# Moving the division by the softmax sum from the attention stage into the loads of the output projection

## The reference

```python
h = _layernorm(x, axis=-1) * (1 + ca) + sa
...
scores = jnp.einsum('bhqd,bhkd->bhqk', q, k) / jnp.sqrt(jnp.float32(D))
scores = jnp.where(causal[None, None], scores, jnp.finfo(x.dtype).min)
attn = jax.nn.softmax(scores, axis=-1)
out = jnp.einsum('bhqk,bhkd->bhqd', attn, v)
out = out.transpose(0, 2, 1, 3).reshape(b, s, H * D)
return out @ Wo
...
x = x + ga * attention(h)
```

## Time and profile before

| | us |
|---|---|
| executions of the kernel before | 2085.73, 2091.81, 2093.32 (median 2091.81) |
| the profiled execution | 2089.15 |
| its span, first to last instruction | 2087.3 |
| mean granted TensorE clock, share of full speed | 0.947 |
| TensorE matmuls busy in the span | 1812.4 (87%) |
| VectorE, ScalarE, GpSimd busy | 1277.5, 1149.3, 953.9 |
| attention lasts, in the span | about 109 to 1425 |
| output projection | about 1425 to 1679 |
| feed-forward | 1679 to the end |

### The profile page before, as it was taken

One profiled execution on the slowest core, in us unless ns is written; L12 is line 12 of the kernel. 1 busy time (PEld: TensorE's weight loads), 2 busy tenths in 40 slices (PEclk: granted clock), 3 DMA queues, 4 the chain that ended last, 5 costly groups with the idle time before them and its releaser, 6 DMA issues. The chain is left out here.

```text
span 2087.3 us, 32037 instructions
## 1 busy us (share of the span) xinstructions
PE 1812.4 (87%) x9585; PEld 1503.0 (72%) x9585; DVE 1277.5 (61%) x2079; ACT 1149.3 (55%) x2307; POOL 953.9 (46%) x773
## 2 busy tenths in 40 slices
PE   8489989979989989989988998984888869999997
PEld 7377778767768777777777886873766647777776
DVE  6367768768767767767777876783222246454543
ACT  4267767767757767767776776783222234233221
POOL 0236556556556556655655665662000014444443
PEclk8799999999999999999999999997999979999999
DMA  6134334243244334333433433435444310101000
GB/s 239 29 89 117 79 102 120 79 113 102 78 111 107 82 95 108 102 90 100 119 89 99 115 81 94 111 88 171 148 149 146 121 56 1 46 1 46 1 26 21
DMA packets 174968, 191.48 MB, mean 92 GB/s; under 512 B 31408, under 2 KB 117688, under 8 KB 174784
## 3 DMA queue, kind: packets, MB, share of 16 engines
q1 hardware_dynamic: 162496, 170.36, 29.2%
q10 hardware_dynamic: 12288, 18.88, 3.1%
HBM read 86.12 MB, written 31.74 MB: 56 GB/s over the span
## 5 line engine op out<-in xcount | busy, mean ns | idle before, releaser
L816 DVE TENSOR_TENSOR p_lo<-ps_b,p_hi 128x512 fp32r<-128x512 f32 x576 | 394.5, 686 | 190.2 <-ACT p_hi L746 186.7
L746 ACT CAST p_hi<-ps_b 128x512 fp32r<-128x512 f32 x576 | 337.4, 588 | 232.1 <-PE ps_b L702 227.0
L759 ACT ACTIVATE p<-ps_b,negm 128x640 f32<-128x640 f32 (+7 forms) x512 | 381.6, 749 | 123.5 <-DVE negm L824 119.2
L824 DVE TENSOR_REDUCE negm<-ps_b 128x1 f32<-128x640 f32 (+7 forms) x512 | 377.4, 747 | 116.4 <-PE ps_b L694 112.5
L702 PE MATMUL ps_b<-ident,p 128*128 128x128 f32 x2304 | 360.5, 280 | 19.4 <-issue 11.0
L692 PE MATMUL ps_b<-k_hh,q_hl 128*128 128x512 f32 (+3 forms) x768 | 273.0, 355 | 82.4 <-DMA q_hl<-rot_x 53.5
L714 PE MATMUL ps_b<-p_hi,v_hl 128*128 128x512 f32 x576 | 280.7, 487 | 14.8 <-ACT o_sb L752 14.2
L702 PEld LDWEIGHTS ps_b<-ident,p 128*128 128x128 f32 x2304 | 255.9, 143 | 51.2 <-issue 16.8
L693 PE MATMUL ps_b<-k_l,q_hl 128*128 128x512 f32 (+3 forms) x768 | 262.5, 354 | 0.0
L898 POOL TENSOR_TENSOR o_sb<-o_sb,rd_all 64x512 f32<-64x512 f32 x128 | 164.2, 1282 | 177.4 <-DMA rd_all<-reciprocals 175.3
L692 PEld LDWEIGHTS ps_b<-k_hh,q_hl 128*128 128x128 f32 x768 | 149.4, 194 | 128.1 <-issue 57.4
(11 more groups left out here) (139 smaller groups left out, 3311.9 us busy)
## 6 DMA issues: line engine op xcount, KB each, us to landing
rot_x<-rot_s SPq DMA_DIRECT2D x320, 64.0 KB, 2.0
q_hl<-rot_s SPq DMA_DIRECT2D x128, 128.0 KB, 2.4
q_hl<-rot_x SPq DMA_DIRECT2D x128, 128.0 KB, 2.4
rd_all<-reciprocals SPq DMA_DIRECT2D x128, 128.0 KB, 3.0
o_low<-o_sb SPq DMA_DIRECT2D x128, 128.0 KB, 2.2
attention_out<-o_sb SPq DMA_DIRECT2D x128, 128.0 KB, 2.5
o_raw<-attention_out SPq DMA_DIRECT2D x32, 512.0 KB, 6.3
wf<-in_L_ffn_w_gate_up ACTq DMA_DIRECT2D x32, 256.0 KB, 3.1
```

The costliest lines, as they stand in the source:

```text
L746: act.copy(p_hi[:, T % P_RING, :], ps[:, T_BANK + T % 2, :]).then_inc(phi_ready, 1)
L759: act.activation(p_32[:, parity, h, column * P:column * P + nk], s, ACT.Exp, bias=negm[:, k:k + 1], scale=1.0, accum_out=den[:, parity, k: ...
L816: dve.tensor_tensor(p_lo[:, T % P_RING, :], ps[:, T_BANK + T % 2, :], p_hi[:, T % P_RING, :].bitcast(F32), ALU.subtract).then_inc(plo_read ...
L824: dve.tensor_reduce(negm[:, k:k + 1], s, AX.X, ALU.max, negate=True).then_inc(max_ready, 1)
```

## The change

In attention GpSimd's multiply, `rd_all` and `spread_den` are gone; the store follows the add and stands one step earlier. The reciprocals of all heads and queries are kept in DRAM, at a place of their own for each. In the projection each piece gets a second ring buffer `o_by`, filled by two DMAs that read the reciprocals of two heads' rows into 64 partitions each; GpSimd multiplies `o_raw` by `o_by` in place, and ScalarE's cast waits for that instead of for the load.

```diff
@@ attention
-        rd_all = sb("rd_all", [D, 512], F32)
...
-        pairs_out = Events(rd_out, [64] * PAIRS, None)
+        pairs_out = [Events(s, [64] * (PAIRS // 2), None) for s in rd_out]
...
+            rden_g = rden_dram.rearrange("(g h) (u i q) -> g u i h q", u=B, g=KVH, q=P)
...
-                blocks_s.await_(sp, g, n)
+                blocks_a.await_(sp, g, n)
...
             def save_den(g, n):
+                big = BIG[n % 4]
                 pairs_flip.await_(sp, g, n)
                 for b in range(P // DEN_COLS):
-                    rows = slice(DEN_COLS * b, DEN_COLS * b + DEN_COLS)
-                    sp.dma_start(rden_dram[n % 2, :, rows], rd_turned[rows.start:rows.start + len(ROWS), n % 2, :]).then_inc(rd_out, 16)
-
-            def spread_den(g, n):
-                if n % 2 == 0:
-                    pairs_out.await_(sp, g, n // 2)
-                row = rden_dram[n // 2 % 2, GQ * (n % 2):GQ * (n % 2) + GQ, :].rearrange("(o h) q -> o (h q)", o=1)
-                sp.dma_start(rd_all[:], row.broadcast_to([D, GQ * P])).then_inc(rd_in[n % 2], 16)
+                    cols = slice(DEN_COLS * b, DEN_COLS * b + DEN_COLS)
+                    to = rden_g[bass.ds(g, 1), n // 4, 7 - big:big + 1:2 * big - 7, :, cols]
+                    sp.dma_start(to.rearrange("g i h q -> (g i) h q"),
+                                 rd_turned[cols.start:cols.start + len(ROWS), n % 2, :]).then_inc(rd_out[n % 2], 16)
...
-                for g, n in body.blocks(T, LAG + 5):
+                for g, n in body.blocks(T, LAG + 4):
                     store(g, n)
                 for g, n in body.pairs(T, 2):
                     save_den(g, n)
-                for g, n in body.pairs(T, 6):
-                    spread_den(g, 2 * n)
-                for g, n in body.blocks(T, LAG + 5):
-                    if n % 2 == 0:
-                        spread_den(g, n + 1)
...
-                               accum_out=den[:, parity, k:k + 1]).then_inc(p_ready, 1)
+                               accum_out=den[:, parity, (k + GQ) % 8:(k + GQ) % 8 + 1]).then_inc(p_ready, 1)
...
-                    pairs_out.await_(dve, g, n - 2)
+                    pairs_out[n % 2].await_(dve, g, n // 2 - 1)
...
-                for g, n in body.blocks(T, LAG + 4):
-                    blocks_a.await_(pool, g, n)
-                    blocks_rd[n % 2].await_(pool, g, n // 2)
-                    pool.tensor_tensor(o_sb[0:D, n % 2, :], o_sb[0:D, n % 2, :], rd_all[:], ALU.mult).then_inc(o_scaled, 1)
@@ project_outputs
+        o_by = sb("o_by", [P, O_RING, PIECE, HALF], F32)
...
+            by_n = rden_dram.rearrange("(k o) (n i t) -> n i o k t", n=NCH, i=2, o=2)
...
                 sp.dma_start(o_raw[:, s % O_RING], ot_n[bass.ds(n, 1), :, i, k].rearrange("n p k t -> (n p) k t")).then_inc(o_in[s % O_RING], 16)
+                for o in range(2):
+                    src = by_n[bass.ds(n, 1), i, o, k].broadcast_to([D, PIECE, HALF])
+                    sp.dma_start(o_by[D * o:D * o + D, s % O_RING], src).then_inc(by_in[s % O_RING], 16)
...
-                    act.wait_ge(o_in[s % O_RING], n * (16 * NPC // O_RING) + 16 * (s // O_RING + 1))
+                    act.wait_ge(o_divided, n * NPC + (s + 1))
...
+            def body(n, first):
+                for s in range(NPC):
+                    slot, turn = s % O_RING, s // O_RING + 1
+                    pool.wait_ge(o_in[slot], n * (16 * NPC // O_RING) + 16 * turn)
+                    pool.wait_ge(by_in[slot], n * (32 * NPC // O_RING) + 32 * turn)
+                    pool.tensor_tensor(o_raw[:, slot], o_raw[:, slot], o_by[:, slot], ALU.mult).then_inc(o_divided, 1)
+
+            chunks(pool, body)
@@ transformer_block
-    rden_dram = dram("reciprocals", (2, len(ROWS), P), F32)
+    rden_dram = dram("reciprocals", (ST + H, T), F32)[ST:, :]
```

More of the change, by code:

```diff
@@ L382, in attention @@
             "s_ready", "max_ready", "p_ready", "t_ready", "phi_ready", "plo_ready", "pv_done")]
-        o_copied, o_added, o_scaled = sem("o_copied"), sem("o_added"), sem("o_scaled")
+        o_copied, o_added = sem("o_copied"), sem("o_added")
         o_shifted, o_out = [[sem("%s%d" % (n, i)) for i in range(2)] for n in ("o_shifted", "o_out")]
@@ L388, in attention @@
             "swapped", "rotated", "qhi_ready", "qlo_ready", "q_placed")]
-        rd_ready, rd_flipped, rd_out = [sem(n) for n in ("rd_ready", "rd_flipped", "rd_out")]
-        rd_in = [sem("rd_in%d" % i) for i in range(2)]
+        rd_ready, rd_flipped = sem("rd_ready"), sem("rd_flipped")
+        rd_out = [sem("rd_out%d" % i) for i in range(2)]
         wf_in, abs_ready, sign_ready, gsum_ready, gscale_ready, above_ready, picked, hat_ready, dif_ready, mag_ready, tern_ready, tern_out = [
@@ L398, in attention @@
         tiles_t, tiles_hi, tiles_lo, tiles_pv = [Events(s, [1] * STEPS, None) for s in (t_ready, phi_ready, plo_ready, pv_done)]
-        blocks_o, blocks_a, blocks_s = [Events(s, [1] * (2 * PAIRS), None) for s in (o_copied, o_added, o_scaled)]
-        blocks_shift, blocks_rd, blocks_out = [[Events(s, [16] * PAIRS, None) for s in pair] for pair in (o_shifted, rd_in, o_out)]
+        blocks_o, blocks_a = [Events(s, [1] * (2 * PAIRS), None) for s in (o_copied, o_added)]
+        blocks_shift, blocks_out = [[Events(s, [16] * PAIRS, None) for s in pair] for pair in (o_shifted, o_out)]
         uses_x, uses_done = [Events(s, [1] * X_BODY, X_HERE) for s in (x_ready, x_used)]
@@ L630, in _ @@
                 sp.wait_ge(o_out[n], 16 * PAIRS * KVH)
+                sp.wait_ge(rd_out[n], 64 * PAIRS // 2 * KVH)
             sp.wait_ge(tern_out, 16 * UNITS * KVH)
@@ L945, with project_outputs @@
 TERNS, GU_TERNS = 6, 4
-def project_outputs(nc, x, wo, tern_gu, tern_p, ot_dram, gates_dram, x2_dram, ident, wo_lo, o_hi, o_lo, gu_b, wp_b):
+def project_outputs(nc, x, wo, tern_gu, tern_p, ot_dram, rden_dram, gates_dram, x2_dram, ident, wo_lo, o_hi, o_lo, gu_b, wp_b):
     with ExitStack() as ctx:
@@ L970, in project_outputs @@
         o_in = [sem("c_o_in%d" % i) for i in range(O_RING)]
+        by_in = [sem("c_by_in%d" % i) for i in range(O_RING)]
+        o_divided = sem("c_o_divided")
         turned, tern_out, id_ready = [sem("c_" + n) for n in ("turned", "tern_out", "id")]
@@ L1535, in transformer_block @@
             wp_b = sb("wp_b", [P, MT * E], BF16)
-            project_outputs(nc, rows, wo, tern_gu, tern_p, ot_dram, gates_dram, x2_dram, ident,
+            project_outputs(nc, rows, wo, tern_gu, tern_p, ot_dram, rden_dram, gates_dram, x2_dram, ident,
                             wo_lo, o_hi, o_lo, gu_b, wp_b)
```

## The result

The changed kernel takes 2163.35 us (median of 4 runs, 2160.93 to 2168.46) beside 2088.93 of the kernel before on the same chip: ratio 1.0359, 95% interval 1.0342 to 1.0377. I had forecast slower, 2108, in a range up to 2128. The sign holds; the size lies outside the range.

A forecast was written before the change was run, and what follows sets the result against it. It took TensorE to be busy and stalled by chains: SP's queue behind GpSimd in attention, load-to-o_lo in the projection. From 2089.15, 31.5 us less in attention and 50.6 more in the projection gave 2108, range 2082 to 2128.

The forecast's parts named there:

- The sign: Whole kernel: slower, 2108 us forecast for the median; chance 0.57 of being slower by over 0.5%.
- The bound: Whole kernel: GpSimd's work alone counts for nothing; SP's queue behind GpSimd decides attention, load-o_hi-o_lo-matmul chains the projection.
- The q wait: Attention: TensorE's seven stalls for q_hl shrink from 7.4 to about 3.9 us, 24.5 less; 3.5 more from the clock.
- The end of attention: End of attention: a spread and a multiply drop out between last add and last store, 3.5 us less.
- The multiply: Projection: GpSimd's 128 x 1024 multiply adds 2.56 us per piece before o_hi, taken as twice a 1281 ns one.
- piece 4: Projection: chain grows 4.5 us per chunk, from multiply 2.56 and two more DMAs with 512 KB, 1.9.
- piece 6: Projection: chain grows 6.4 us per chunk, from 1 MB more 2.7, multiply 2.56 and slowed o_lo 1.1.
- the even chain: Projection: pieces 2, 4, 6 form the slower chain and decide each chunk, 10.9 us more in each of four.
- my lower bound of 28: Projection: least loss, 28 us, if the new loads land with o_raw and only the multiply counts.
- rival B: Whole kernel: attention's gain and projection's loss cancel, as only the multiplies lengthen the chains; 2086 to 2100 us, chance 0.30.
- loads that cost double: Projection: upper bound of the loss, 66 us, if loads and ports cost double.
- Rival D: Projection: each o_lo on a chain waits for the next piece's whole multiply, shared port; 16 us, 2124; chance 0.12.

The follow-up runs named there:

- m3: Changed kernel with each DRAM row of reciprocals made longer, so the runs of an o_by load lie 18 KB apart instead of 16; 2092.61 us, ratio 1.0010.
- k1: Changed kernel with reciprocals laid out in DRAM so that the four 1 KB runs of an o_by load lie 2 KB apart, not 16; 2090.50 us, ratio 1.0018.
- m1: k1 with the ternary loads one piece later on SP's queue; 2061.99 us, ratio 0.9857.
- e1: Changed kernel without the o_by loads and without the multiply, so the division is left out; 2057.42 us, ratio 0.9847.
- e2: Changed kernel with o_by loaded only for the first four pieces and all 32 multiplies kept; 2091.47 us, ratio 1.0005.
- e4: Changed kernel with o_by loads as large, but each partition reads its own row of the attention output; 2095.28 us, ratio 1.0030.
- e6: Changed kernel with each partition reading four 1 KB runs of its own from the reciprocals' tensor, 64 KB apart; 2088.10 us, ratio 1.0009.
- h1: Changed kernel with each ternary unit loaded one piece later on SP's queue; 2098.75 us, ratio 1.0065.
- k2: Changed kernel with each o_by load reading one 4 KB run of true values, written by eight half-size stores per pair instead of four; 2145.50 us, ratio 1.0282.

## Why the prediction was right in sign and wrong in size

- **The sign, right by luck.** With the address pattern cured the change makes no difference (m3: ratio 1.0010, 0.9994 to 1.0027; k1: 1.0018, 1.0000 to 1.0037). What made it slower is a term that the forecast did not have.
- **The bound, right.** GpSimd's busy time counted for nothing, and each stage was set by the chain I named, though in the projection by its other half.
- **The q wait, right in the long waits, too large as a sum.** Forecast: seven waits of 3.5 to 4 us instead of 7.4, 24.5 less. The trace has seven of 3.2 to 4.7, 28.5 in all instead of 50.7, so 22.2 less. But six small ones stand beside them that were not there before, 6.3 us; the q wait shrank by 15.9.
- **The rest of the 28.6 us.** The waits of L707 for o_sb fell by 8.4, which I had not seen; other small ones grew by some 3. TensorE's busy time fell by 7.5 (1156.8 against 1164.3, the granted clock 0.98 instead of 0.96), where I had put 3.5. That is within what one execution differs from the next: in the twelve profiled ones with this attention (k1 and m1 among them) it lies between 1150.5 and 1165.4. Two rows of the line that waits for o_sb, before and after:

```profile
PE ps_b L714 <- ACT o_sb L752: 14.2, 22, 1.5
```

```profile
PE ps_b L707 <- ACT o_sb L745: 5.8, 14, 0.7
```

- **The end of attention, right.** Without the division the gap before the projection is 18.2 instead of 22.9: 4.7, forecast 3.5. e1 gains 32 us where this part of the sum said 31.5, and that close a match is in part luck: in its trace 24.0 come from attention, 4.7 from the gap and 4.0 from the projection, for which I had nothing.
- **The multiply, right in duration.** 2378 ns in the median; I had taken 2.56 us from twice.
- **The failed step** is, at piece 4, "512 KB more to move, 1.3 us at the 390 GB/s that the busiest stretch reaches", and its like at piece 6 (1 MB, 2.7 us). I counted the o_by loads as ordinary bytes. They land in 11.0 us, and while they run the ternary loads take 8.5 instead of 3.0 and o_raw 8.8 instead of 6.3. The trace put 83 us from one chunk's piece to the next chunk's (its start 1530.0, then 1612.8 and 1696.8), where it had 58 to 60: 24 more per chunk, not 10.9. At piece 5 of the second chunk 8.7 us pass between the last issue of o_by and the multiply. The stalls moved as well, from pieces 4 and 6 to pieces 3 and 5: I had the even chain decide, and it is the odd one, in m3 too (pieces 3 and 5 stall 6.1 to 7.2 us in its last three chunks, 4 and 6 at most 0.3). The projection came out at 361.5 us by the stretches where I had said about 300, the waits for o_lo at 137.2 where I had said 90 to 110.
- **Two errors against one another.** With the address pattern cured (m3) the projection and its gap are 30.0 longer than before (266.0 + 24.4 against 237.5 + 22.9), where I had forecast 50.6, near my lower bound of 28, which counts the multiplies alone. Ordinary loads cost hardly anything on top of the multiply: e2, with almost none, has 290.1. So what I had priced for the loads was too much for ordinary ones and far too little for these. The cured change is rival B, to which I gave 0.30: 2092.6, no difference. That it meets the bound so nearly is chance, as other pieces stall than I had said. The pattern adds 70.3 on top (334.5 + 26.2 less 290.4), and for that I had no term and no rival. My bound for "loads that cost double" was 66 in all; 100.3 came.
- **Rival D, the port.** In the changed kernel o_lo takes 1224 to 1227 ns in all 32 pieces: no collision, since a piece was never early enough. Once pieces are early it does occur: in e2 o_lo has a mean of 1523 and a longest of 3283 ns, which is 1.2 plus most of a multiply. The Trainium skill, "SBUF — State Buffer", section "Who interferes with whom", says that these two kinds of instruction exclude one another; e2 agrees. What decided was whether the next piece had landed. It is at most 9.5 us of VectorE's time there (32 times 0.30), not the 34 of the multiply. Before a stall of TensorE it stands at piece 6 of three chunks, where o_lo takes 2.27 to 2.41 us, 1.0 to 1.2 more than alone; I had taken 1.1. The rest, as far as the trace tells, is the added link; no run separates the two.

The part that was foreseeable: the trace of before had a load of this kind (the spread of rd_all, 128 KB, lands in a median of 3.0 us), but it repeats a single run of 2 KB and cannot show what four runs 16 KB apart do. A bound for an unseen form of load should have been taken from both sides, and its upper end was not the bandwidth.

## What to carry to other kernels

Before a row of DRAM is spread over partitions many times, look at the distance between the runs that one transfer repeats; padding the row length is a change of one line and was worth 71 us here. Read DMA share and GB/s together: here more share at nearly the same rate (0.45 to 0.65, 149 to 155) meant slow accesses; the same bytes at a better distance moved at 193. And where an awaited event stands in a queue ahead of a load that a chain needs, moving it one place behind that load can be worth more than taking work off any engine: 38 us here, for the kernel before.

## What the runs showed of the hardware

- A load of 256 KB to 64 partitions that repeats four 1 KB runs lands in 11.0 us with the runs 16 KB apart, 6.8 at 18 KB, 6.6 at 2 KB, and 6.6 as one run of 4 KB; with runs of its own for each partition 6.1 and 6.6 (e4, e6). These medians hold for this order of loads; with pieces ahead they are 11.2 at 16 KB (h1) and 8.5 at 2 KB (m1).
- It slows others in flight: 16 of the 24 ternary loads of 256 KB go from 3.0 to 8.5 us in the median and back to 2.9 once the runs are 2 KB apart. Issuing an o_by load took SP's queue 0.83 us in the median, with 0.61 in k1.
- Halving a small store did not make its issue cheaper: those of 0.5 KB (k2) hold SP's queue 0.62 us in the median, those of 1 KB (k1) 0.64.
- A subtraction of two SBUF tiles of 128 x 1024 takes VectorE 1.22 us alone and up to 3.28 beside a GpSimd multiply (e2).
